# The junction between two passes: ks summed before the last moment product, kv added by diagonal blocks, the first two out products in a row

## What is computed

```
h  = layernorm(x) * (1 + ca) + sa
q  = elu(h @ Wq.T + bq) + 1
k  = elu(h @ Wk.T + bk) + 1
v  = h @ Wv.T + bv
KV = sum over all rows of k x v, per head
ks = sum over all rows of k
attn = (q . KV) / (q . ks + 1e-6)
x  = x + ga * (attn @ Wo.T + bo)
x  = x + gb * experts(layernorm(x) * (1 + cb) + sb)
```

## Time and profile before

| | us |
|---|---|
| median of 3 runs | 1280.54 |
| lowest, highest | 1279.32, 1280.56 |
| the profiled execution | 1278.65 |
| its span in the profile | 1276.9 |
| TensorE busy | 1225.7 (96% of the span) |
| VectorE, GpSimd, ScalarE busy | 1025.5, 558.1, 537.6 |

### The profile page before, as it was taken

The page is one execution under the profiler, slowest core; times in us unless marked ns, Lnnn a source line. Parts: engine busy times, 40 slices in busy tenths (PEclk is TensorE's granted clock), DMA queues, the critical chain, the costliest instruction groups (busy, mean ns, idle before and its releaser), DMA issues.

```text
span 1276.9 us, 18483 instructions
## 1 busy us (share of the span) xinstructions
PE 1225.7 (96%) x5742; PEld 997.7 (78%) x5742; DVE 1025.5 (80%) x2275; ACT 537.6 (42%) x1117; POOL 558.1 (44%) x401
## 2 busy tenths in 40 slices
PE   7999999999999999999789999999999999999998
PEld 5777787788778888886578888788888888888787
DVE  5898999888898888786677787777877777778764
ACT  2444444545445455553343343433434343343431
POOL 1333433433334444433355464544536455464531
PEclk9999999999999999999899999999999999999999
DMA  8445444443334444433321322313132231322201
GB/s 212 145 149 177 150 126 141 152 141 123 109 110 130 125 132 130 129 113 83 83 67 50 100 71 78 99 52 100 59 92 83 66 100 57 93 78 72 83 17 50
DMA packets 131681, 131.64 MB, mean 103 GB/s; under 512 B 12328, under 2 KB 86480, under 8 KB 131584
## 3 DMA queue, kind: packets, MB, share of 16 engines
q1 hardware_dynamic: 131584, 130.47, 33.4%
HBM read 80.62 MB, written 49.81 MB: 102 GB/s over the span
## 4 chain that ended last, share of the span: by engine, by line
PE 58%; DVE 15%; POOL 11%; issue 7%; ACT 7%; DMA 1%; SPq 0%; DVEq 0%; POOLq 0%; ACTq 0%
PE ps L1475 18%; PE ps L1476 18%; PE ps L1480 17%; POOL xb L679 6%; POOL rrs L718 3%; PE ps L1662 2%; POOL rstd L711 2%; DVE x L1303 2%; DVE mod L1047 2%; DVE xT_lo L1310 1%; DVE zk L1199 1%; DVE zk L1211 1%; DVE qf L1184 1%; ACT exp_k L805 1%; ACT exp_q L798 1%
## 5 line engine op out<-in xcount | busy, mean ns | idle before, releaser
L705 POOL TENSOR_TENSOR cn<-c,half 128x16 f32<-128x16 f32 x32 | 104.2, 3256 | 281.3 <-DVE c L1338 281.3
L667 POOL TENSOR_TENSOR ks_acc<-ks_acc,zk 128x512 f32<-128x512 f32 x64 | 83.1, 1299 | 219.1 <-DVE zk L1211 219.1
L798 ACT ACTIVATE exp_q<-qf 128x512 f32<-128x512 f32 x64 | 40.5, 632 | 171.0 <-DVE qf L1184 171.0
L671 POOL TENSOR_TENSOR xn_lo<-xn,xn_hi 128x512 fp32r<-128x512 f32 x64 | 109.6, 1712 | 0.0
L1475 PE MATMUL ps<-g_hi,qT_hi 128*128 128x512 f32 x256 | 104.7, 409 | 4.9 <-ACT qT_hi L843 4.9
L1475 PE MATMUL ps<-wk_hi,xT_hi 128*128 128x512 f32 x256 | 102.8, 402 | 5.3 <-ACT xT_hi L774 5.0
L1475 PE MATMUL ps<-wq_hi,xT_hi 128*128 128x512 f32 x256 | 102.5, 400 | 1.7 <-DVE qf L1184 1.2
L1475 PE MATMUL ps<-v_hi,xT_hi 128*128 128x512 f32 x256 | 102.9, 402 | 0.0
L1475 PE MATMUL ps<-k_hi,xn_hi 128*128 128x512 f32 x256 | 102.3, 400 | 0.0
L1476 PE MATMUL ps<-g_lo,qT_hi 128*128 128x512 f32 x256 | 101.6, 397 | 0.0
L1476 PE MATMUL ps<-wq_lo,xT_hi 128*128 128x512 f32 x256 | 101.4, 396 | 0.0
(11 more groups left out here) (240 smaller groups left out, 3284.0 us busy)
## 6 DMA issues: line engine op xcount, KB each, us to landing
xin<-_attn_hidden_states_dram SPq DMA_DIRECT2D x64, 256.0 KB, 3.1
q_scratch<-qf SPq DMA_DIRECT2D x64, 256.0 KB, 3.2
xin<-_attn_hidden_states_dram SPq DMA_DIRECT2D x32, 512.0 KB, 4.3
q_in<-q_scratch SPq DMA_DIRECT2D x128, 128.0 KB, 2.9
out_dram<-qf SPq DMA_DIRECT2D x64, 256.0 KB, 2.0
xn_scratch<-xn SPq DMA_DIRECT2D x62, 256.0 KB, 2.1
xq<-xn_scratch SPq DMA_DIRECT2D x248, 64.0 KB, 2.5
wm_in<-in_L_wmod_dram SPq DMA_DIRECT2D x4, 1024.0 KB, 5.9
```

The lines of the kernel that those rows point to most:

```text
L667: nc.gpsimd.tensor_tensor(ks_acc[:], ks_acc[:], kf[:, s, :], ALU.add).then_inc(ks_done, 1)
L671: nc.gpsimd.tensor_tensor(quarters(xn_lo[:, 1 - s, :]), natural(xn[:, 1 - s, :]), quarters(f32(xn_hi[:, 1 - s, :])), ALU.subtract).then_in ...
L705: nc.gpsimd.tensor_tensor(cn[:].rearrange("p h e -> p (h e)"), c2[:].rearrange("p h e -> p (h e)"), half[:], ALU.pow).then_inc(cn_done, 1)
L798: nc.scalar.activation(exp_q[:, 1 - s, :], zq[:, 1 - s, :], ACT.Relu, scale=-1.0).then_inc(rq_done, 1)
```

## The change

- TensorE: the q product of tile 62 moves behind the moment product of tile 62, and that of tile 63 behind `kv`. The sum of `ks` stands ahead of the last moment product. Each block of M signals by itself (`m_block`) when it is complete. The four out products of pairs 0 and 1 stand in a row ahead of the turns of pair 0; the warm-up matmuls between them are gone. The first out product waits for each `g` block by itself.
- VectorE: `mt` blocks 0 and 2 here, 1 and 3 on ScalarE. `ks_row` is gone; `outer` is one instruction of 128x128 where it was four. `kvm` is cleared by GpSimd beforehand, and only its diagonal blocks are added, in four instructions of 32 partitions, where four instructions of 128x256 stood. Work of pairs 0 and 1 stands between the junction's own.
- GpSimd: `kvm` cleared and `xb` of pair 0 made ahead of the last addition to `ks_acc`; `qks` of pairs 0 and 1 and `xb` of pair 1 ahead of pass B's loop. `xb` has two slots.
- SyncE: x and q of pairs 0 and 1 are loaded after the q store of tile 61; the q stores of tiles 62 and 63 follow, with x of pair 1 between them. The load of pair 2's q waits for the store of tile 63.
- Tiles are placed anew in memory so that these buffers are free earlier; `g2` and `g3` go to banks 3 and 4.

The core of the diff (the lines in the common order of both kernels and the placement of tiles are left out):

```diff
@@ SyncE
-                if i == T:
+                if i == T - 2:
                     sp.wait_ge(xn_done, T)
                     bx_load(0)
-                    sp.wait_ge(q_psum, T)
+                    sp.wait_ge(weights_ready, 1)
...
-            sweep_tiles(step, -2, T)
+            sweep_tiles(step, -2, T - 1)
+            q_store(T - 2, 0)
+            sp.wait_ge(xb_done, 1)
+            bx_load(1)
+            q_store(T - 1, 1)
@@ VectorE, the junction as it stands after
+            def scaled_moment(b):
+                dve.wait_ge(m_block, b + 1)
+                nc.vector.tensor_scalar(quarters(mt[b]), natural(ps[:, b, :]), ca4_col[:, b:b + 1], None,
+                                        ALU.mult).then_inc(mt_dve, 1)
+
+            q_biased(T - 2, 0)
...
+            dve.wait_ge(ksq_done, KB)
+            taken_by(nc.vector.tensor_tensor(groups(outer[:]), groups(ks_q[:]), over(bvp_col[:], [P, KB, DH]), ALU.mult), "ks")
+            scaled_moment(0)
+            q_feature(T - 2, 0)
+            scaled_moment(2)
+            denominators(0)
+            inverses(0)
+            full("kv")
+            dve.wait_ge(kv_cleared, 1)
+            for i in range(KB):
+                last = nc.vector.tensor_tensor(kvm[quarter(i), :, quarter(i)],
+                                               bank("kv").rearrange("p (b n) -> p b n", n=P)[quarter(i), :, quarter(i)],
+                                               groups(outer[:])[quarter(i)], ALU.add)
+            taken_by(last, "kv")
+            scaled_q(0)
+            turned_q(0)
+            q_biased(T - 1, 1)
...
@@ TensorE
+            sweep_tiles(step, 0, T - 1)
             pe.wait_ge(ks_done, T)
             sum_rows("ks", ks_acc[:])
+            moment(T - 1, 1)
             pe.wait_ge(zk_done, T)
...
             last.then_inc(prep_psum, 1)
+            q_product(T - 1, 1)
+            pe.wait_ge(prep_taken, TAKE["kv"] + 1)
```

More of the change, by code:

```diff
@@ L1453, in step_b @@
                     variances(j - 1)
[L1454 removed]
+                if j == 0:
+                    residual(1, 0)
+                if live(j + 1, J) and j > 0:
                     qT_low(j + 1, 0)
@@ L1602, in step @@
-                    last.then_inc(m_done, 1)
-                prepare(i, 1)
-                if live(i, T):
-                    if isinstance(i, int) and i == 0:
-                        pe.wait_ge(wlo_done, 2 * KB)
-                    wait_count(pe, zq_done, i)
-                    three(bank_q, [(xT_hi[:, s, b * P:(b + 1) * P], xT_lo[:, s, b * P:(b + 1) * P],
-                                    wq_hi[:, b, :], wq_lo[:, b, :]) for b in range(KB)], True, True).then_inc(q_psum, 1)
-            sweep_tiles(step, 0, T)
+                    moment(i - 1, 1 - s)
```

274 lines of the change are left out of this document (141 added, 133 removed).

## The result

| | before | after |
|---|---|---|
| median, us | 1280.55 | 1271.68 |
| lowest, highest | 1279.32, 1280.94 | 1270.75, 1273.58 |
| the profiled execution | 1278.65 | 1273.58 |
| its span in the profile | 1276.9 | 1271.9 |

The ratio is 0.9937, 95% interval 0.9924 to 0.9949. A second comparison of the same two kernels gave 0.9932 (0.992 to 0.9945), 9.5 us.

A forecast was written before the change was run, and what follows sets the result against it. TensorE, busy 96% of the span, was taken as the bound, with winnable idle time only behind 606 us. Terms 1.7 + 0.7 + 1.3 = 3.7 us took the median from 1280.54 to 1276.8; range 1273.2 to 1280.6.

The forecast's parts named there:

- step 7: The rest: warm-ups gone, ks_row, three outer and a small copy, and the 7 us gap behind F: counted 0.
- F: The prediction's mark: end of pair 0's second fused product, 633.06 us before, start of the steady stretch, forecast 629.4.
- Step 1: End of pass A: new order ends the last moment product at 593.9, not 595.6; kv could start 2.8 us earlier.
- Step 2: VectorE between the mt blocks: qf of tile 62 held by GpSimd's qks until 595.2; of 2.8 us, 0.6 left.
- rival A: The clock: three new TensorE gaps of about 2.4 us halve it; gain 0.9 to 2.3, about 1278.9; chance 0.27.
- Step 3: Junction: kvm additions take 1.3 us, covered by tile 63's q product; g products end 606.3 instead of 608.7.
- Step 4: Pair 0: xb holds qz until 603.2, first out product ends 611.75; some 6 us won, most lost again later.
- Step 5: Two chains to pair 0's rstd: the queue through tile 63's store and qks ends last, 621.2, 1.7 us earlier.
- Step 6: From rstd to F: 0.7 us from less work between pair 0's turns, 1.3 us from full clock behind them.
- C: Pair 0's rstd stands behind slow store, load and qks of pair 2: slower than before, 1282.5; chance 0.08.
- D: Change doesn't reach F: another in-order VectorE or ScalarE instruction eats the rest; 0 to 2 us, 1279.5; chance 0.13.
- B: No holding: qf or qz miss GpSimd's operations; gain 7.3 us, 1273.2; chance 0.12, part ways included.

The follow-up runs named there:

- place_only: Kernel before, its own instruction order, with all tiles where the change puts them: median 1277.97 us, ratio 0.999 (0.998 to 1.0).
- place_g: Kernel before with g_hi and g_lo where the change has them, qT_hi and qT_lo at a third place: step 20.108 us, out product 2.780 us.
- after_3: The changed kernel unedited, run for a third trace: median 1271.82 us.
- qf_behind: Changed kernel with the features of tile 62 behind the second mt block on VectorE, not between the two: 1268.65 us, ratio 0.9914.
- fill_gap: The 1268.65 us kernel qf_behind with pair 1 reordered on ScalarE, GpSimd and VectorE to fill the 7 us gap: 1268.37 us, ratio 0.9908.
- after_again: The changed kernel unedited, once more beside the kernel before: 1271.24 against 1280.77 us, ratio 0.9932.
- rstd_first: Changed kernel with rstd of pair 0 ahead of qks of pair 2 on GpSimd: 1271.7 us, ratio 0.9939.
- undo_out: Changed kernel with pair 1's two out products and their casts and residuals back in the next step, without warm-ups: 1273.87 us, ratio 0.9958.

## Why the prediction was wrong, point by point

**The step that failed is step 7, "the rest", counted at nothing.** It named warm-ups, `ks_row` and the 7 us gap, and left the tiles placed anew out of the working altogether, though the text on the change lists them. The change and the kernel before differ by 3.0 us behind F, some 0.1 us in each of some 30 steps, and place_only gives 2.7 against the mean of the three traces of before (2.4 against the first) with no other edit. The prediction's sentence that "the end moves by as much as the start of the steady stretch" rests on this zero, and it is false. With 3.0 in its place the sum is an estimated 6.7 us and 1273.8, inside the range. The trace before held a hint that is plain only afterwards: the out product takes 2.780 us there and the value product, with as many matmuls of the same width, 2.730. That is 0.05 us for each of two out products a step, an estimated 0.1 x 30 = 3 us; it is no firm bound, since place_g could slow the value product as well.

**The sum for the junction came out by errors that cancelled.** 3.7 us were forecast, 3.4 separate the two profiled executions at F, 4.4 the means of three traces each. Of the traces after, after_3 is the easiest to hold against the prediction: its m is 40.85 where before has 40.87, so its times need no shift. Its values stand second below. The terms:

- *Step 1, order in pass A:* right. `ks` was to start near 590.0; it started at 590.19 in the clock of before, and at 590.10. The second `mt` block was to be complete at 596.4; it was at 596.26 and 596.17. The first `xb` did not hold TensorE up.
- *Step 2, qf held:* right in mechanism and end (2.08 us long), and qf_behind shows that it costs what the text said. The Trainium skill's rule on the shared pair (SBUF — State Buffer, "Who interferes with whom") agrees with this row, and with both holds of fill_gap. `kv` was to end at 600.0. In after it ended at 601.3, since the clock fell at its gap of 1.88 (5.02 us): this is rival A's mechanism. In after_3 and after_again it did not fall there (3.39 us), and `kv` ended at 599.6 in after_3.
- *Step 3, kvm:* 1.19 us for the four additions, where 1.3 was taken between bounds; g 3.59 and 3.60, where 3.5 was. The q product of tile 63 covered the additions.
- *Step 4, qz held by xb:* not in after, where `kv` was too late for it; in after_3 and after_again yes, with 2.39 and 2.40 us. The first out product was to end at 611.75 and ended at 610.95 and 610.42, so up to here the forecast was 0.8 to 1.3 us too late.
- *Step 5, the queue to rstd:* from the features of tile 63 to `qks` of pair 2 the prediction had 6.45 us, and 6.51 and 6.47 were measured. The features came earlier, so `rstd` started at 619.9 and 619.3 and not at 621.2, 1.3 to 1.9 us earlier than forecast. Nor was it what TensorE waited for: moved ahead of `qks` it won nothing (rstd_first). What was late next was TensorE itself.
- *Step 6, from rstd to F:* 8.2 us were forecast and 9.7 and 9.8 measured. The out products of pair 1 ran partly at half clock behind their gap of 2.3 us and took 7.0 to 7.2 us in every trace of the change, instead of the 5.58 of full clock, and turn (0, 0) had to wait for them. Without that loss of 1.6 they would have been done at 621.8 in the clock of before, an estimate, and from `rstd` at 619.9 the turn could have come at 621.8 too, by the 1.9 us that it took in the earlier trace rows. So the loss at half clock went into the turn in full. The part about the clock behind the turn was right (both turns at 0.60 and 0.63, F 4.21 behind turn (0, 1) as in pair 1), and undo_out shows it from the other side.

So `rstd` was 1.3 to 1.9 us better than reckoned, and the stretch behind it 1.5 to 1.6 worse, by a clock fall that the sum had left to rival A. That the two nearly cancel, and F lies within 0.3 us of 629.4 (629.63 and 629.10), is luck. The chain in the sum was wrong in its last part.

**The base.** The sum was made against an execution at 1278.65 and carried over to the median as it was. The kernel before has no one way through: m to F varies by 2.2 us between its traces, and the first step by 1.4 between the layouts with its order. The execution that was read had a granted clock of 0.995, which none of the 30 executions without a kept trace reached. Against an ordinary execution the change saves more than against this one, and the 1.5 to 2 us that the two terms leave open probably lie here; which falls of the clock they are is not shown.

**Rivals.** A (the clock) named the right mechanism. Of its three gaps, the one at pair 1 brought a fall on the path in all three traces, the one inside `kv` in one of three, and that in front of the first out product, 1.2 us at most, in none. But it expected the time to be lost from the sum, and the sum had 1.3 to 1.9 us to spare. C (slower by the trip through memory) did not come: `qks` of pair 2 started at 617.6 in the clock of before, 4.9 us ahead of the point from which it would have decided. D came in part: `rstd` was 3.0 us earlier than before (622.94 to 619.9), turn (0, 0) only 1.5, since TensorE itself, and not an instruction on VectorE or ScalarE, ate the rest. B's half, `qz` not held, came true in after, for another reason, and not in after_3 or after_again.

**What the range lacked.** It took every unknown from the junction. The largest unknown lay in a part of the change that adds, removes and moves no instruction, and the next in how the execution that was read compares with the others.

## What to carry to other kernels

Where tiles are placed anew, compare products of the same shape on different tiles in the trace before: a few hundredths of a microsecond in a loop that leaves its engine no gap are multiplied by the loop, and here outweighed each term of a careful sum. When an instruction moves to the front, ask of the next one in line not only what data it waits for but whether its own engine is free; a gain in the queue ahead of a busy engine is none. And read more than one trace before a step is called right or wrong: whether `qz` was held differs between executions of the same kernel. A chain behind a busy stretch that looks fixed may be an order written for the steady state: the first steps of a pipeline can have an order of their own, but only if all the chains of the next step are moved with it (1268.4 with one, 1265.2 with both).
